# Decoder layer, self-attention: score products over 64 rows per head, a new order of the TensorE steps, and two of five copies moved to ScalarE

## The reference, cut to what matters

```python
x = x + _L0_attn_ref(_layernorm(x), ...)     # 8 batches of 512 tokens, width 512, float32
x = x + _L0_xattn_ref(...)                   # untouched
x = x + _L0_ffn_ref(...)                     # untouched

# _L0_attn_ref: 16 heads (H) of 64 (HD); one window of 512 tokens is the whole batch
h = x * rsqrt(mean(x * x) + EPS) * norm_w
q, k, v = proj(w_q), proj(w_k), proj(w_v)
ll = einsum('bhnqd,bhnkd->bhnqk', qw, kw) * HD ** -0.5
ll = where(tril, ll, NEG)                    # causal
scores = h @ scorer_w + scorer_b             # the 128 highest tokens count a second time
attn = softmax(concatenate([ll, lg]))
o = attn @ v;  return x + o @ w_out
```

## Time and profile before

| | |
|---|---|
| time, median of 3 runs | 2294.71 us (2288.63 to 2298.39) |
| profiled execution, its own time | 2289.59 us |
| its span, first to last instruction | 2287.9 us |
| TensorE matmul busy | 2112.8 us, 92% of the span |
| VectorE, ScalarE, GpSimd busy | 58%, 37%, 31% |
| mean granted TensorE clock | 0.947 |

### The profile page before, as it was taken

One profiled execution on the slowest core, in us unless ns is written; L12 is line 12 of the kernel. 1 busy time (PEld: TensorE's weight loads), 2 busy tenths in 40 slices (PEclk: granted clock), 3 DMA queues, 4 the chain that ended last, 5 costly groups with the idle time before them and its releaser, 6 DMA issues. The chain is left out here.

```text
span 2287.9 us, 36708 instructions
## 1 busy us (share of the span) xinstructions
PE 2112.8 (92%) x12029; PEld 1651.3 (72%) x12029; DVE 1333.4 (58%) x3141; ACT 837.5 (37%) x1537; POOL 697.9 (31%) x1060
## 2 busy tenths in 40 slices
PE   4999999999999999999999999987899999878899
PEld 4886886788688688678768858855788888854443
DVE  3673485277178268447627817734887878745401
ACT  2442443344144144234324414414544444313210
POOL 4320321131142042122113113215776767520000
PEclk9999999999999999999999999997887879769899
DMA  4101101100200211111011011012013212150000
GB/s 138 38 29 58 37 29 33 61 29 29 65 29 29 66 29 37 33 51 38 25 60 38 25 60 38 29 56 63 27 59 132 67 49 67 51 202 0 1 0 19
DMA packets 112665, 110.13 MB, mean 48 GB/s; under 512 B 12083, under 2 KB 78643, under 8 KB 111976
## 3 DMA queue, kind: packets, MB, share of 16 engines
q1 hardware_dynamic: 111848, 105.74, 14.6%
q0 software_dynamic: 640, 2.10, 0.2%
HBM read 89.99 MB, written 17.83 MB: 47 GB/s over the span
## 5 line engine op out<-in xcount | busy, mean ns | idle before, releaser
L338 POOL TENSOR_TENSOR idle<-ones 128x4 f32<-128x4 f32 x171 | 36.1, 211 | 1129.8 <-PE pj_bank L607 812.2
L438 ACT ACTIVATE probs<-s_bank,nmax 128x512 f32<-128x512 f32 (+3 forms) x512 | 249.6, 526 | 346.5 <-DVE nmax L558 245.0
L708 PE MATMUL o_bank<-vals,probs_t 128*128 128x65 f32 x2560 | 323.0, 269 | 0.0
L708 PEld LDWEIGHTS o_bank<-vals,probs_t 128*128 128x128 f32 x2560 | 311.0, 192 | 3.3 <-DVE probs_t L566 3.3
L558 DVE TENSOR_REDUCE nmax<-s_bank 128x1 f32<-128x512 f32 (+2 forms) x384 | 184.4, 508 | 199.2 <-PE s_bank L685 195.7
L732 PE MATMUL pj_bank<-w_o,o_t 128*128 128x512 f32 x512 | 226.9, 604 | 6.0 <-ACT o_t L446 6.0
L566 DVE COPY probs_t<-pt_bank 128x512 f32<-128x512 f32 x320 | 217.7, 680 | 3.6 <-PE pt_bank L693 3.6
L693 PE MATMUL pt_bank<-ident,probs 128*128 128x128 f32 x1280 | 194.8, 275 | 14.6 <-DVE probs_t L566 14.4
L732 PEld LDWEIGHTS pj_bank<-w_o,o_t 128*128 128x128 f32 x512 | 98.3, 193 | 129.9 <-issue 129.9
L681 PE MATMUL s_bank<-k_twice,q_both 128*128 128x512 f32 (+3 forms) x512 | 189.5, 372 | 0.0
L416 ACT ACTIVATE vals<-pj_bank,twice 128x512 f32<-128x512 f32 x64 | 44.0, 688 | 350.9 <-PE pj_bank L607 338.2
(11 more groups left out here) (263 smaller groups left out, 4427.2 us busy)
## 6 DMA issues: line engine op xcount, KB each, us to landing
wq_raw<-in_L_attn_w_q SPq DMA_DIRECT2D x65, 256.0 KB, 3.0
wk_raw<-in_L_attn_w_k SPq DMA_DIRECT2D x65, 256.0 KB, 3.8
xb<-in_x SPq DMA_DIRECT2D x9, 1024.0 KB, 5.5
xt<-x SPq DMA_DIRECT2D x36, 256.0 KB, 2.8
probs<-in_x SPq DMA_DIRECT2D x32, 256.0 KB, 2.7
x<-probs SPq DMA_DIRECT2D x32, 256.0 KB, 2.0
am<-in_L_ffn_attention_mask SPq DMA_DIRECT2D x8, 1024.0 KB, 5.4
out<-x SPq DMA_DIRECT2D x32, 256.0 KB, 2.1
```

The lines of the kernel that those rows point to most:

```text
L438: ins = nc.scalar.activation(probs[:, i % 2, c0:c0 + nk], s_bank[i % 2][:, c0:c0 + nk], ACT.Exp, bias=nmax[:, i % 4, n:n + 1])
L708: ins = nc.tensor.matmul(o_bank[slot][:, o0:o0 + VW], probs_t[:, i % 2, c0 + P * kt:c0 + P * kt + P], vals[:, kt, 2 * p + h, :], start=(kt ...
```

## The change

1. **Scores.** Query and key parts are stored as they come, both heads in 128 rows: `q_hi`, `q_lo`, `k_hi`, `k_lo`. Each head's scores are three products over its own 64 rows (head 0 in rows 0 to 63, head 1 in rows 64 to 127), the heads alternating, head 0 into one PSUM bank and head 1 into the other. A new step "rows" does query block 3 of both heads (6 products and 2 masks), then blocks 0 and 2 (12 and 4), then block 1 (6 and 2). ScalarE and VectorE store each part with one instruction over 128 rows.
2. **Order.** A pair has three "rows" steps. Between two of them stand two or more other TensorE steps; the q and k projections are cut in halves of 6 products ("q_half", "q", "k_half", "k"). A "rows" step waits for the exponentials of all units before it, as it writes both banks. `probs` gets four places. "stats", "dot" and "rank" are cut in pieces ("above", "tied") and spread over the pairs.
3. **Copies.** ScalarE does the copy to `probs_t` for units 1 and 3 of each pair (`ON_ACT`), VectorE for units 0, 2 and 4.
4. The zeroing of `k_lo` at the start is gone.

```diff
+PROBS = 4
+ON_ACT = (1, 3)
+def row_blocks(j):
+    return [[(3, 0, 512)], [(0, 0, 128), (2, 128, 384)], [(1, 0, 256)]][j]
...
+    plan += [("q_half", 0), ("q", 0), ("q_lo", 0), ("k_half", 0), ("k", 0), ("k_lo", 0)]
     plan += [("v", i) for i in range(2 * TT - 2, 2 * TT)]
...
+    for p in range(NPAIR):
+        u, more = UNITS * p, p + 1 < NPAIR
+        plan += [("rows", 3 * p), ("s", u), ("s", u + 1), ("t", u - 2), ("pv", u - 3)]
+        plan += [("q_half", p + 1)] * more + [next(extra, None), ("t", u - 1), ("pv", u - 2)]
+        plan += [("rows", 3 * p + 1), ("s", u + 2), ("s", u + 3)] + [("q", p + 1)] * more
+        plan += [("t", u), ("pv", u - 1)] + [("q_lo", p + 1), ("k_half", p + 1)] * more + [next(extra, None)]
+        plan += [("rows", 3 * p + 2), ("s", u + 4)] + [("k", p + 1)] * more + [("t", u + 1)]
+        plan += [("k_lo", p + 1)] * more + [("pv", u), ("ot", p - 1), ("t", u + 2), ("pv", u + 1), next(extra, None)]
+    plan += [("t", NU - 2), ("pv", NU - 3), ("ht", 0), ("t", NU - 1), ("pv", NU - 2), ("ht", 1), ("ht", 2),
+             ("pv", NU - 1), ("ht", 3), ("ot", NPAIR - 1)]
...
+                        if first:
+                            pe.wait_ge(p_ready, b * NU + first)
+                        blocks = row_blocks(j)
+                        terms = ((q_hi, k_hi), (q_lo, k_hi), (q_hi, k_lo))
+                        for n, (t, c0, nk) in enumerate(blocks):
+                            for m, (queries, keys) in enumerate(terms):
+                                for h in range(2):
+                                    nc.tensor.matmul(s_bank[h][:, c0:c0 + nk],
+                                                     queries[head_rows(h), p % 2, P * t:P * t + P],
+                                                     keys[head_rows(h), p % 2, 0:nk],
+                                                     start=(n == 0 and m == 0), stop=False, skip_group_check=True)
+                        for h in range(2):
+                            for n, (t, c0, nk) in enumerate(blocks):
+                                ins = nc.tensor.matmul(s_bank[h][:, c0 + nk - P:c0 + nk], ident_b[:, :],
+                                                       causal_b[:, :], start=False, stop=(n == len(blocks) - 1),
+                                                       skip_group_check=True)
+                            if j < 2 or h == 1:
+                                ins.then_inc(s_ready, 1)
...
+                    if kind == "t" and i % UNITS in ON_ACT:
+                        slot, ready = pt(b, (kind, i))
+                        act.wait_ge(pt_ready, ready)
+                        if i >= 2:
+                            act.wait_ge(pv_ready, b * NU + i - 1)
+                        nc.scalar.copy(probs_t[:, i % 2, :], pt_bank[slot][:, :]).then_inc(ts_act, 1)
```

More of the change, by code:

```diff
@@ L117, in attention_plan @@
-    plan.append(("ot", NPAIR - 1))
+    extra = [("stats", t) for t in range(TT)] + [None] * 2 + [("dot", t) for t in range(TT)] + [("score", 0)]
+    extra += [(k, t) for t in range(TT) for k in ("above", "tied")]
+    extra = iter([None] * 3 + extra)
+    plan = [("v", i) for i in range(2 * TT - 2)]
+    plan += [("q_half", 0), ("q", 0), ("q_lo", 0), ("k_half", 0), ("k", 0), ("k_lo", 0)]
+    plan += [("v", i) for i in range(2 * TT - 2, 2 * TT)]
+    for p in range(NPAIR):
[6 more added lines that the diff above has]
+        plan += [("k_lo", p + 1)] * more + [("pv", u), ("ot", p - 1), ("t", u + 2), ("pv", u + 1), next(extra, None)]
@@ L376, in _ @@
                 for kind, i in plan:
-                    if kind == "stats":
+                    if (kind, i) == ("stats", TT - 1):
                         pl.wait_ge(h_ready, b * TT + TT)
@@ L421, in _ @@
                         act.wait_ge(pj_ready, ready)
[L422 to L430, removed]
+                        if kind == "q":
+                            nc.scalar.activation(q_hi[:, i % 2, :], pj_bank[slot][:, :], ACT.Copy,
+                                                 scale=HD ** -0.5).then_inc(qk_hi, 1)
+                        else:
+                            nc.scalar.copy(k_hi[:, i % 2, :], pj_bank[slot][:, :]).then_inc(qk_hi, 1)
                     if kind == "s":
@@ L464, in stats, with dot @@
                 ins.then_inc(stats_ready, 1)
-            def dot(n):
+            def dot(n, t):
                 dv.wait_ge(h_ready, n * TT + TT)
[L469 to L472, removed]
+                step(nc.vector.tensor_tensor_reduce(junk[:, :], xb[:, t, :], sw[:, :], 1.0, 0.0, ALU.mult,
+                                                    ALU.add, score[:, t:t + 1]))
+                if t < TT - 1:
+                    return
                 nc.vector.tensor_scalar(score[:, :], score[:, :], sbias[:, 0:1], None, ALU.add).then_inc(score_ready, 1)
@@ L515, in _ @@
                 nc.vector.memset(carrier[:, 1 + i:2 + i], 0.0).then_inc(at_one, 1)
-            stats(0)
+            for t in range(TT):
+                stats(0, t)
             dv.wait_ge(small_in, 64)
@@ L523, in _ @@
                 normed(None, 0, c)
-            dot(0)
+            for t in range(TT):
+                dot(0, t)
             score_row(None, 0)
             for t in range(TT):
-                rank(None, 0, t)
+                above(0, t)
+                tied(None, 0, t)
             with dv.Fori(0, B) as b, done.loop(b, 2 * TT + 2 * TT + 1 + NU, B):
@@ L584, in _ @@
                     if kind == "stats":
-                        stats(b + 1)
+                        stats(b + 1, i)
                     if kind == "dot":
-                        dot(b + 1)
+                        dot(b + 1, i)
                     if kind == "score":
                         score_row(b, b + 1)
-                    if kind == "rank":
-                        rank(b, b + 1, i)
+                    if kind == "above":
+                        above(b + 1, i)
+                    if kind == "tied":
+                        tied(b, b + 1, i)
                     if kind == "ht":
```

142 lines of the change are left out of this document (57 added, 85 removed).

## The result

| | before | after |
|---|---|---|
| time, median | 2293.9 us (2288.63 to 2298.39, 9 runs) | 2282.75 us (2280.12 to 2286.49, 9 runs) |
| ratio, 95% interval | | 0.995 [0.9939, 0.9961] |
| profiled execution; its span | 2289.59; 2287.9 us | 2280.48; 2278.7 us |

The change makes the kernel faster by 0.5%, 11 us. The prediction had the sign right and forecast 25 us. It also took anything within 11.5 us for no change (chance 0.23); the median's 11.2 lies just inside that, though the interval is clear of 1.

A forecast was written before the change was run, and what follows sets the result against it. The prediction took TensorE's own work to bound the attention stage. Scores at -2.1 and waits at -1.1 us a batch, times 8, gave -25 us: 2269 us, with a range of 2236 to 2320 (the forecast's own 2240 to 2290).

The forecast's parts named there:

- Scores after: TensorE's score products, loads, masks and switches per pair in the new form; middle taken between two cases, -0.26 us a pair.
- rival 2: On TensorE, each change between full and half height costs a switch, four a pair at 0.085 us: 2291 us; chance 0.12.
- both side by side: Score case where the two heads' products and loads both overlap on TensorE: 2.67 us a pair, -0.72.
- For loads ... I take the middle, 0.084: Half-height load on TensorE priced at 0.084 us, between 0.056 (two together) and 0.111 (one by one).
- The waits: TensorE's waits across middle pairs, eighth value projection, pair 1 and last pair: -1.1 us a batch in sum.
- The 0.46 before the transposes: TensorE's wait in each middle pair at a mask before transposes, for a bank's copy: 0.46 us lost, forecast to go.
- `k_lo`'s 1.03: TensorE's wait for `k_lo` at the eighth value projection: 1.03 us a batch, forecast to go.
- The last pair's three waits: TensorE waits in the last pair's gaps, without projections as cover: 1.26, 1.4 and 0.86 us; +1.7 with the tail.
- Rival 1: Half-height loads go one by one on TensorE while products overlap, +0.20 us a pair: 2299 us; chance 0.16.
- Rival 3: Within a half, a load isn't hidden under the product before it, +0.46 us a pair: 2316 us; chance 0.08.
- rival 4: Nothing runs side by side on TensorE, so added columns cost +1.21 us a pair: 2364 us; chance 0.10.
- Rival 5: ScalarE's in-order queue becomes the new wait, half a microsecond later in each pair: 2297 us; chance 0.08.

The follow-up runs named there:

- half_height_once: Kernel before, with the fifth of 12 products in each q and k projection reading only 64 rows: 2342.19 us, ratio 1.0215.
- masks_first: Changed kernel, with the masks of each "rows" step ahead of its products instead of behind them: 2284.61 us, 0.9971 of the kernel before.
- full_rows: Changed kernel, with every score product reading all 128 rows, so both heads mix in each score: 2355.44 us, 1.0286 of the kernel before.
- heads_in_turn: Changed kernel, with three products of head 0, then three of head 1, in place of alternating heads: 2285.99 us, 0.9973 of the kernel before.
- masks_between: Changed kernel, with block 0's masks put between the products of blocks 0 and 2: 2298.64 us, 1.0031 of the kernel before.

## Why the prediction was right in sign and off in size

Its sum, set against the traces, us a batch (TensorE's -0.26 a pair put where it belongs):

| part | forecast | measured | read from |
|---|---|---|---|
| six middle pairs | -4.2 | -2.64 | first score of pair 2 to that of pair 8: 98.26, 95.62 |
| pair 1 | +0.5 | +0.7 | value projection to first score of pair 2: 14.83, 15.54 |
| last pair and tail | +1.4 | +1.9 | 19.42, 21.36 |
| eighth value projection | -1.0 | -1.3 | output projection to it: 54.53, 53.22 |
| sum | -3.2 | -1.3 | x 8: -26, -10 |

**The step that failed is in "Scores after": the sum prices a change between half and full height at nothing, and the runs show 0.72 us a pair for six of them.** The prediction knew the price as rival 2, with a chance of 0.12. A second term was off the other way: "For loads ... I take the middle, 0.084". Both parts of the case "both side by side" came true, 0.056 for a load included, which the prediction priced at 2.67 us of scores a pair against 3.39, -0.72. With that and still nothing for the height its forecast would have been 2240, 43 us off; that it was off by 14 is luck, one error covering part of the other. Rival 2 came true beside it and took the 0.72 back: three ways in (0.93 for 0.81 behind "pv" twice, 0.32 for 0.23 behind the k half, together 0.33), three ways out to the masks (0.10, 0.09, 0.09), and 0.11 on a first product that was counted as plain (behind the k half). That is 0.72 of the 0.77 that the traces show (3.44 for 2.67); 0.05 is not assigned. Rival 2 had four changes at 0.085 and let two ways in pass as already paid by the type switch. There are six. A change of height has its hole also where a type switch stands (0.93 for 0.81); the two share only the long first product, which either brings alone (half_height_once, masks_first). So TensorE's own work came out at +0.05 a pair, not -0.26: 0.31 x 64 = 20 us of gain that isn't there. The waits, -1.1 a batch in the forecast, came out at -1.7, which gives 5 us back.

**The waits, right.** The 0.46 before the transposes is gone in every middle pair, `k_lo`'s 1.03 is gone, and 0.3 more at the seventh value projection (its first product starts 0.38 us after its neighbour in the trace before, the next 0.34 after it, and both 0.23 in the one after), pair 1 pays 0.7 for 0.8. The last pair's three waits are 1.18, 1.1 and 0.71 for 1.26, 1.4 and 0.86. They sum to less than expected, yet the stretch is longer than expected: the tail does not absorb them as my walk had it. Why, no run shows.

**Rivals 1, 3 and 4, fallen.** Loads go two at a time (0.11 for a pair of them), they are hidden within a half, and products overlap; full_rows shows what nothing side by side costs, 1.48 for 0.91 and 2355 us, near the 2364 of rival 4. That case would have made a loss of the change.

**Two readings were off** without moving the forecast. Of the profiled execution before, 1.7 us lie outside its span (2289.59 and 2287.9), not 2.3. And the clock is not quite full in the self-attention: the tenths of the earlier trace rows hide three low-clock stretches, 5.1 us.

**Rival 5, fallen in the middle pairs, true at the end.** The pair is 15.87 with and without ScalarE's copies; in the last pair they cost 0.85.

**Where the gain of the change went:** on TensorE into the changes of height, which cost the 0.72 us a pair that the new form was to save over the stacked one; and of some 4.3 us of waits taken away in a batch (3.0 in the middle pairs, 1.3 at the value projection) 2.5 came back in pair 1 and the last pair, where too little or no projection work covers the exponentials.

## What to carry to other kernels

Products over half the rows of the array run two at a time, loads too, but every passage between half and full height costs TensorE 0.1 us and lengthens the product behind it: count the passages, put the half-height products together, and weigh both against what running side by side saves. A schedule that spreads dependent steps with filler work has to say what the filler is in the first and the last round. The best filler is work of the bounding engine alone: output projection products in the last pair brought 37 us, while turns that ScalarE and VectorE must store brought a loss.

## What the runs showed of the hardware

- Neighbouring halves of the array take their products as if each had a queue: in heads_in_turn, head 1's first product starts 10 ns after head 0's first, ahead of two that come before it in the program, and the pair stays at 15.88 us. The Trainium skill (TensorE: Matmul & The Clock Gate, "Part 3: Packing small matmuls — row/col tiling") has matmuls start strictly in program order. The trace differs, and it decides.
- A passage between 64 and 128 rows: 0.38 us out and back between products of 512 columns, 0.23 in masks_between, where the masks stand between.
- TensorE falls to 1.2 GHz for 3.4 us in or right behind some last pairs, which hold waits of a microsecond (566.0, 0.53 of full clock); a stretch costs 1.7 us in the output projection. Once the waits are filled, no batch of a trace has one there. But the traces of masks_between and masks_first, with these waits unfilled (21.65 and 21.24 us for the last pair), have none there either, so the waits alone do not bring it.
